# Post-norm decoder layer on one core: the exp of the attention scores by side

## The reference

```python
x = layernorm(x + linear_attention(x))          # state = 0.99 state + 0.01 v k^T, one step per token
q, k, v = heads(x @ w_q.T + b_q), heads(ctx @ w_k.T + b_k), heads(ctx @ w_v.T + b_v)   # 16 heads of 16
x = layernorm(x + softmax(q @ k.T / sqrt(16)) @ v @ w_o.T + b_o)
q, k, v = heads3(x @ W_qkv + b_qkv)
attn_out = softmax(q @ k.T / sqrt(16)) @ v
comb = top-2 of softmax(x @ W_gate + b_gate), zero elsewhere        # 8 experts
moe_out = sum over experts of comb * (x @ W_expert + b_expert)
x = layernorm(x + attn_out + moe_out)
```

## Time and profile before

| | us |
|---|---|
| median of 3 runs | 1267.0 (1264.37 to 1269.11) |
| profiled execution, its own time | 1266.94 |
| its span, first to last instruction | 1265.0 |
| PE busy | 1220.8 (96%) |
| DVE busy | 902.8 (71%) |
| ACT busy | 771.1 (61%) |
| POOL busy | 366.0 (29%) |

### The profile page before, as it was taken

How to read it: one execution, slowest core, us unless ns; L and a number is a source line. 1 busy time by engine, 2 the same in 40 slices (tenths; PEclk the granted TensorE clock), 3 DMA queues, 4 the chain that set the end, 5 groups by cost and what they waited for, 6 DMA issues and landing times.

```text
span 1265.0 us, 19962 instructions
## 1 busy us (share of the span) xinstructions
PE 1220.8 (96%) x6936; PEld 601.8 (48%) x6936; DVE 902.8 (71%) x1836; ACT 771.1 (61%) x1072; POOL 366.0 (29%) x471
## 2 busy tenths in 40 slices
PE   8889999999999999999999999999999999999998
PEld 4433444544555445454554545454454534544443
DVE  2577886677777787777776777767877787667772
ACT  2255556666675765756657665666657576655664
POOL 6410103211621134320522206221153204430261
PEclk9899999999999999999999999999999999999999
DMA  7825034313233342233333143332223333303300
GB/s 254 135 43 94 18 52 68 51 29 76 50 69 52 51 85 42 51 45 70 68 67 61 20 74 68 68 52 45 51 42 51 52 52 52 68 2 52 52 19 18
DMA packets 50243, 74.92 MB, mean 59 GB/s; under 512 B 8536, under 2 KB 20320, under 8 KB 49888
## 3 DMA queue, kind: packets, MB, share of 16 engines
q1 hardware_dynamic: 48896, 72.72, 32.8%
q10 hardware_dynamic: 1248, 0.92, 0.4%
HBM read 18.04 MB, written 4.19 MB: 18 GB/s over the span
## 4 chain that ended last, share of the span: by engine, by line
PE 83%; DVE 7%; ACT 5%; issue 3%; DMA 1%; ACTq 0%; POOL 0%; SPq 0%; DVEq 0%
PE ms L451 38%; PE op L451 17%; PE sc L451 15%; PE mx L451 9%; DVE maxes L928 3%; ACT probs L759 2%; PE ms L557 2%; PE ms L502 1%; ACT moe L752 1%; PE ms L552 1%; DMA qs<-q_parts 1%; DMA w_ident<-in_ident 1%; DVE k_parts L838 0%; ACT x L777 0%; DVE heads L901 0%
## 5 line engine op out<-in xcount | busy, mean ns | idle before, releaser
L928 DVE TENSOR_REDUCE maxes<-mx 128x1 f32<-128x512 f32 x1024 | 657.4, 683 | 215.3 <-PE mx L451 213.4
L759 ACT ACTIVATE probs<-sc 128x1024 f32<-128x1024 f32 x512 | 524.3, 1024 | 373.8 <-PE sc L451 368.3
L1131 POOL TENSOR_TENSOR x<-x,moe 128x256 f32<-128x256 f32 x256 | 187.4, 732 | 687.0 <-ACT moe L752 666.5
L451 PE MATMUL op<-probs,v 128*32 128x512 f32 x2048 | 273.6, 606 | 2.9 <-ACT oT L697 2.5
L451 PE MATMUL sc<-qs,ks 50*128 50x512 f32 x1024 | 256.7, 497 | 11.9 <-ACT probs L759 10.3
L451 PEld LDWEIGHTS sc<-qs,ks 50*128 50x128 f32 x1024 | 95.4, 183 | 308.4 <-ACT probs L759 231.5
L451 PE MATMUL mx<-ks,qs 48*128 48x512 f32 x1024 | 209.0, 402 | 10.9 <-DVE maxes L928 8.9
L752 ACT ACTIVATE moe<-ms,comb 128x256 f32<-128x256 f32 x256 | 106.8, 472 | 22.1 <-PE ms L451 22.1
L451 PEld LDWEIGHTS mx<-ks,qs 48*128 48x128 f32 x1024 | 97.7, 187 | 20.8 <-DVE maxes L928 14.7
L451 PE MATMUL ms<-we_hi,x2T_hi 128*128 128x512 f32 x256 | 93.7, 447 | 2.5 <-DVE shift_r L892 1.3
L451 PEld LDWEIGHTS op<-probs,v 128*32 128x32 f32 x2048 | 40.5, 108 | 96.4 <-issue 95.0
(11 more groups left out here) (131 smaller groups left out, 1264.8 us busy)
## 6 DMA issues: line engine op xcount, KB each, us to landing
ks<-k_parts SPq DMA_DIRECT2D x192, 128.0 KB, 4.2
qs<-q_parts SPq DMA_DIRECT2D x189, 128.0 KB, 4.6
xT_s<-in_xT SPq DMA_DIRECT2D x8, 512.0 KB, 3.8
x_s<-in_x SPq DMA_DIRECT2D x8, 512.0 KB, 4.0
ctxT_s<-in_ctxT SPq DMA_DIRECT2D x8, 512.0 KB, 4.2
out<-x SPq DMA_DIRECT2D x7, 512.0 KB, 2.9
qs<-shift_r SPq DMA_DIRECT2D x128, 8.0 KB
probs<-in_we SPq DMA_DIRECT2D x1, 1024.0 KB, 7.1
```

The source lines that it names most:

```text
L451: return nc.tensor.matmul(dst, lhsT, rhs, start=first, stop=last, skip_group_check=True)
L759: nc.scalar.activation(probs[:, (2 * s + h) % 3, :, :], sc[:], ACT.Exp).then_inc(exp_out, 1)
L928: nc.vector.tensor_reduce(maxes[:, g % 2, at:at + 1], mx[:, i % 3, :], AX_X, ALU.max).then_inc(max_out, 1)
L1131: nc.gpsimd.tensor_tensor(x2[:, n % 2, t, :], x2[:, n % 2, t, :], moe[:, k % 2, j * D:j * D + D], ALU.add).then_inc(acc, 1)
```

## The change

The exp of a half is issued as two instructions, one per side, each with 128 x 512 elements. Each waits for its own side's score product, each raises `exp_out`. Each score product waits for the exp of its own side of the half before, and each raises `score`. So both semaphores rise by two per half, and the other waits on them (the DMA queue's and the values products') count double.

```diff
@@ the DMA queue, before it overwrites a part of ks or qs
-                    sp.wait_ge(score, 2 * 8 * (e - RING + 1))
+                    sp.wait_ge(score, SIDES * 2 * 8 * (e - RING + 1))
@@ TensorE, scores(s, h)
-                if 2 * s + h >= 1:
-                    pe.wait_ge(exp_out, 2 * s + h)
                 if kb == 0 and h == 0:
                     pe.wait_ge(shift_in[g % 2], 16 * SIDES * (g // 2 + 1))
                 for side in range(SIDES):
                     at = 64 * side
-                    last = mm(sc[:, side, :],
+                    if 2 * s + h >= 1:
+                        pe.wait_ge(exp_out, SIDES * (2 * s + h - 1) + side + 1)
+                    mm(sc[:, side, :],
                               ks[at:at + ROWS + SHIFT, e % RING, 2 * (g % 2) + h, kb * P:kb * P + P].bitcast(F32R),
-                              qs[at:at + ROWS + SHIFT, e % RING, 2 * (g % 2) + h, :].bitcast(F32R), True, True)
-                last.then_inc(score, 1)
+                              qs[at:at + ROWS + SHIFT, e % RING, 2 * (g % 2) + h, :].bitcast(F32R), True, True).then_inc(score, 1)
@@ TensorE, values(s)
-                pe.wait_ge(exp_out, 2 * s + 2)
+                pe.wait_ge(exp_out, SIDES * (2 * s + 2))
@@ ScalarE, exps(s, h)
-                act.wait_ge(score, 2 * s + h + 1)
                 if s - 1 + h >= 1:
                     act.wait_ge(pv, s - 1 + h)
-                nc.scalar.activation(probs[:, (2 * s + h) % 3, :, :], sc[:], ACT.Exp).then_inc(exp_out, 1)
+                for side in range(SIDES):
+                    act.wait_ge(score, SIDES * (2 * s + h) + side + 1)
+                    nc.scalar.activation(probs[:, (2 * s + h) % 3, side, :], sc[:, side, :], ACT.Exp).then_inc(exp_out, 1)
```

## The result

The changed kernel takes 1280.98 us (median of 4, 1279.87 to 1282.74) against 1267.82 us for the kernel before on the same chip: a ratio of 1.0109, 95% interval 1.0086 to 1.0133. Run again with the experiments it took 1281.87 us, 1.0109 [1.0087, 1.0131]. It is slower by 1.1%, some 13 to 14 us, where I had forecast 5. A step of 0.001 in it is about 1 us, so such a comparison is no finer than that. The profiled execution took 1280.77 us and its span is 1279.0 us, 14.0 over that of before.

What follows compares the result with a forecast made beforehand. TensorE's own work was taken to bound the kernel, with the exp barely hidden in first halves. Terms 6.0 - 0.6 + 0.9 + 1.2 - 0.8 - 1.5 = +5.2 us gave 1272 us; range 1264 to 1286.

Steps and rivals of the forecast that it cites:

- pulled-apart rival: Score products: a wait between the two, or its cost on TensorE, lengthens each half; 1281 us likelier, up to 1323; chance 0.1.
- dearer exps: ScalarE: second exp overlaps less or costs more than the copies; about 1297 us at +0.165, halfway 1284; chance 0.2.
- the sum with a pair 0.093 us longer: Exp pair at the skill page's price instead of +0.065: sum some 7 us larger, about 1279 us.
- TensorE's own step: First halves: TensorE's work takes 1.65 to 1.67 us, the loop through the exp 1.62, hiding the exp by 0.04 to 0.05.
- Side 0 gains nothing in first halves: First halves: side 0's exp wait ends over 0.4 us early, but values products stand ahead on TensorE; no gain.
- The loop to side 1: First halves: 1.685 us against 1.66 of own work, side 1 0.025 us late, 240 times: +6.0 us.
- the tenth that I took (-0.6): Where the last-ending chain leaves TensorE, 17% of the span, side 1's delay can be swallowed: a tenth, -0.6 us.
- Half B: +0.9: A slot's second half, where the exp's cover is gone: side 1 0.065 us later at about 14 waits, +0.9 us.
- take-outs +1.2: ScalarE empties the units' bank after the exp, so 0.065 us later: 30 waits x 0.04, +1.2 us.
- Gains, -0.8 and -1.5: Last six slots shorter through side 0's early release, -0.8 us; where the exp queued on ScalarE, -1.5 us.
- Extra waits and increments: 0: Each score product's own wait and increment on TensorE costs 0; upper end 0.11 us per half, 56 us.
- Faster: Rival, every first half: early side 0 weight loads shrink the step after the values; 1262 or 1255 us; chance 0.08.

Runs made afterwards that it cites:

- e5: Kernel before, with idle matmul pairs of 48 rows x 256 columns added ahead of the max products in first halves: 1290.30 us, 1.0180.
- e1: Changed kernel, with the wait for the side's scores named ahead of the wait for the values products in the exps: 1269.63 us, 1.0024.
- e2: Kernel before, with its exp's two waits exchanged, values products first and scores second: 1273.94 us, 1.0051.
- e6: Changed kernel, with the same idle matmul pairs in first halves as e5: 1296.28 us, 1.0211.
- e3: As e1, but both score products wait for both exps of the half before: 1277.00 us, 1.0074.
- e4: Kernel before with one exp of 1024 columns, but a wait and an increment for each score product: 1268.89 us, 1.0022.
- e7: As e1, with each side's exp in two instructions of 256 columns, four to a half: 1298.71 us, 1.0232.
- e8: Change kept only in the last 12 halves and two of each 64; elsewhere one exp, semaphores raised by two at once: 1271.63 us, 1.0033 to kernel before.
- e10: As e8, but unsplit halves raise their semaphores by one and the waits count accordingly: 1266.79 us, 0.9995 to kernel before.

## Why the prediction was right, and where it was short

The direction, the mechanism and the place hold, and so does the range; the size was less than half of what came. That the range held is in part luck: the forecast itself was 1269 to 1276 us, and 1281 lies in the room that was left for the rivals. The pulled-apart rival named 1281, dearer exps 1284 at half their price, and the sum with a pair 0.093 us longer came to 1279, each by something that is not what the runs show.

- *TensorE's own step, 1.65 to 1.67 us, sets first halves, and the weight loads' 231.5 us of waits are no price.* Right. Those waits fell to 225.1 us in a slower kernel; the filler in e5 cost its 0.12 us in each ordinary first half.
- *The pair of exps is 0.065 us longer.* Right: 1.085 against 1.023 us, +0.062. By the price in the Trainium skill, ScalarE: Activation LUTs, What ACT_TABLE_LOAD costs, it would have been 0.093, an estimate. The trace is below that page: a half exp is 0.597 us, nearer to the copies' 0.594 than to the 0.613 estimated from its figures.
- *Side 0 gains nothing in first halves, side 1 waits for the second exp.* Right: side 0 at the old step (1665 ns), side 1 0.052 us after the second exp.
- *The loop to side 1 is 1.62 + 0.065 = 1.685 us.* This is the term that was mis-sized. It is 0.496 + 0.097 + 1.085 + 0.052 = 1.73 us. I carried over the 0.045 us from the scores' end to the exp's start, which the exchange of the two waits turned into 0.097. Side 1 is 0.067 us late, not 0.025: in the trace 13.3 us for the first halves instead of 6.0. Of what first halves lose, second halves give back nearly a fifth rather than the tenth that I took (-0.6): of each 64, the halves 23, 35, 45, 53 and 61 are 0.35 us shorter together, against 1.93 in the first halves. e1 takes just this away and comes to 1.0024; e2 adds just this to the kernel before and comes to 1.0051. The exchange stood in the diff, and the view of line 758 would have shown which wait stood alone; only its price was in no row.
- *Half B: +0.9, take-outs +1.2.* Second halves pay together 1.6 us over the trace, 2.5 of which is the step at half clock, and -0.9 in the halves 64 to 383, gains and what they give back in it. The payers are there: half 29 of each 64, with the short unit, is 0.047 us longer, and the halves 5, 9, 11, 21, 25 and 37 0.03 to 0.05 each, 63 0.11. That second halves pay for a late exp is seen in e2, +1.4 us in that stretch, and in e6 against e5. Both terms are of the right sort; their exact sizes over the whole trace stay open.
- *Gains, -0.8 and -1.5.* In the last six slots only the last two came near the 3.11 forecast, with 3.10 in e1 and 3.15 in the change, from 3.24; the slots before them lost more than that, and the six together are 0.2 us longer in the change and 0.1 shorter in e1, not 0.8. The whole early release is worth some 3 us (e3 against e1), against the 2.3 that I gave it.
- *Extra waits and increments: 0.* Right for TensorE's own step (e4). That increments follow each other is so, but the 27 ns fall on the waiter (e4), and where it has no slack, in some second halves, they count: e4 is about 2 us over the kernel before. In the change the first exp waits for side 0's increment alone.
- The rivals: dearer exps, no. The pair pulled apart: it is, in 250 halves, but as an effect of the late second exp and not by its waits; where the exp is hidden (e4, e6) it stays whole. Faster: no.

## What to carry to other kernels

Before splitting an instruction on a loop, compare the loop with the other work of the same step to 0.01 us: here 0.045 us of slack stood between "free" and the full price of every further nanosecond, in 250 places. When waits are rewritten, keep the one that comes last in time on the instruction itself: here by naming it first, and by letting the waiting instruction raise its own semaphore by one, since the exp that raised by two carried no wait. Compare medians only after a look at the granted clock of the runs: it moved e3 by 4 us and e7 by 5. A delay that starts with one of two concurrent matmuls shows in no list of waits; look at the time that the pair takes together.

## What the runs showed of the hardware

- A wait that stands as an instruction of its own on ScalarE starts what follows 0.05 to 0.06 us later than the same wait carried by the instruction: 97 against 37 ns (change and e1), 106 against 45 (e2 and before), 91 against 41 (e8 and e10).
- An exp that raises its semaphore by two carries no wait; both of its waits stand ahead of it (e8, 481 times). A score product that raises by two shows no delay: the wait for it ends 46 ns after it (e8), against 52 ns for one that raises by one (the change).
- Two score products that raise a semaphore by one each start the exp that waits for both 27 ns later than one increment on the last (68 against 41 ns, e4 and before).
- A score product that waits starts 0.052 to 0.057 us after the end of the exp it waits for (52 ns in the change and e1, 55 in e2 and e3, 57 in half 29 of each 64 in the kernel before).
- The granted clock sets single steps: a step at 201 us takes 6.7 us in the change, where the clock falls to half, and 4.1 in the kernel before at full clock.
- Exps of 1024, 512 and 256 columns, one, two and four in a row, take 1.023, 1.085 and 1.215 us for the same data.
